# Channel norm once per token through memory, gates loaded a pair per slot, and residual tile loads on ScalarE's queue, in a hand-pipelined metaformer block

## What is computed

```python
def _ln_c(v, eps=1e-06):                 # over the 64 channels, per token
    m = jnp.mean(v, axis=1, keepdims=True)
    s = jnp.var(v, axis=1, keepdims=True)
    return (v - m) / jnp.sqrt(s + eps)

def _L0_conv_ref(x, ...):
    for s in (0, 2):
        xs = jnp.roll(x, (-s, -s), axis=(1, 2)) if s > 0 else x
        outs = [_window_attend(xh, ...) for xh in (xs[:, :32], xs[:, 32:])]
        if s > 0: outs = [jnp.roll(o, (s, s), axis=(1, 2)) for o in outs]
        results.append(jnp.concatenate(outs, axis=1))
    return results[0] + results[1]

# _window_attend: qkv = qkv_w @ xh; 4x4 windows, 8 heads of 4 channels;
#   softmax(q k^T * scale + bias) v + depthwise3x3(v)
x = x + _L0_conv_ref(_ln_c(x), qkv_w, lepe_w, bias_table)
t = tokens(x)
t = t + ffn(_ln_t(t))    # router softmax, top 2 of 8 experts, x @ expert_w + expert_b
```

## Time and profile before

| what | value |
|---|---|
| median of 3 runs | 3749.16 us (3746.48 to 3774.52) |
| the profiled execution | 3730.37 us |
| its span, first to last instruction | 3728.5 us |
| busy: TensorE, VectorE, GpSimd, ScalarE | 86%, 86%, 79%, 60% |
| mean granted TensorE clock | 0.923 of full speed |
| bytes moved by DMA | 432.05 MB, mean 116 GB/s |

### The profile page before, as it was taken

One profiled execution on the slowest core, in us unless ns is written; L12 is line 12 of the kernel. 1 busy time (PEld: TensorE's weight loads), 2 busy tenths in 40 slices (PEclk: granted clock), 3 DMA queues, 4 the chain that ended last, 5 costly groups with the idle time before them and its releaser, 6 DMA issues.

```text
span 3728.5 us, 203806 instructions
## 1 busy us (share of the span) xinstructions
PE 3199.5 (86%) x82757; PEld 1956.7 (52%) x82757; DVE 3190.4 (86%) x6174; ACT 2233.5 (60%) x4514; POOL 2942.7 (79%) x5385
## 2 busy tenths in 40 slices
PE   3889989988898888898889888888889888989884
PEld 1655555555555555555555555555555555555541
DVE  2789989998999989998889988888889988889983
ACT  2676666666666656665566656665556666666640
POOL 3988878888888878887788878877788878788860
PEclk8999999999999999999899999999899989999996
DMA  1245455555455545555545555545455545455545
GB/s 27 60 97 126 117 123 121 129 120 122 118 127 121 124 109 129 115 127 115 120 110 127 122 117 121 125 111 122 113 120 125 124 115 123 114 116 126 125 104 126
DMA packets 415302, 432.05 MB, mean 116 GB/s; under 512 B 129984, under 2 KB 395888, under 8 KB 414320
## 3 DMA queue, kind: packets, MB, share of 16 engines
q1 hardware_dynamic: 248432, 304.94, 36.0%
q0 software_dynamic: 165888, 113.57, 12.9%
HBM read 245.79 MB, written 58.98 MB: 82 GB/s over the span
## 4 chain that ended last, share of the span: by engine, by line
PE 36%; SPq 23%; issue 15%; DVE 14%; DMA 5%; ACT 3%; POOL 2%; DVEq 0%; ACTq 0%; POOLq 0%
SPq L397 13%; PE bank L628 8%; PE bank L564 7%; DVE lepe L899 4%; SPq L429 4%; PE bank L549 3%; PE bank L641 3%; PE bank L584 2%; SPq L455 2%; DVE gx L887 2%; PE bank L633 2%; DMA gate_rows<-gateT 2%; DVE row_max L907 2%; DMA z<-fin 2%; PE bank L653 2%
## 5 line engine op out<-in xcount | busy, mean ns | idle before, releaser
L504 POOL DMA_DIRECT2D vx<-vt x3072 | 1561.7, 517 | 414.1 <-PE bank L633 403.3
L628 PEld LDWEIGHTS bank<-probT,vx 128*32 128x32 f32 x36864 | 824.6, 189 | 464.5 <-issue 452.8
L628 PE MATMUL bank<-probT,vx 128*32 128x16 f32 x36864 | 886.3, 234 | 159.2 <-issue 144.0
L493 POOL DMA_DIRECT2D kx<-k_sb x1536 | 741.0, 489 | 229.5 <-issue 102.8
L564 PEld LDWEIGHTS bank<-kx,qx 32*32 32x32 f32 x36864 | 584.9, 110 | 443.6 <-issue 441.3
L564 PE MATMUL bank<-kx,qx 32*32 32x64 f32 x36864 | 689.3, 223 | 133.3 <-issue 111.1
L899 DVE SCALAR_TENSOR_TENSOR lepe<-vpad,lepe_sb,lepe 128x384 f32<-128x384 f32 x960 | 673.5, 702 | 0.8 <-issue 0.8
L718 ACT ACTIVATE prob<-prob 128x512 f32<-128x512 f32 x576 | 367.4, 638 | 288.1 <-DVE prob L912 285.0
L887 DVE TENSOR_TENSOR gx<-gate_wide,yn_pair 128x768 f32<-128x768 f32 x384 | 397.4, 1036 | 112.9 <-PE bank L549 62.1
L523 POOL TENSOR_TENSOR lepe_p<-lepe_p,tap_sb 128x384 f32<-128x384 f32 x384 | 434.9, 1133 | 32.7 <-issue 11.3
L912 DVE TENSOR_TENSOR prob<-bank,row_max 128x512 f32<-128x512 f32 x576 | 398.4, 692 | 16.7
(11 more groups left out here) (87 smaller groups left out, 4517.8 us busy)
## 6 DMA issues: line engine op xcount, KB each, us to landing
gate_wide<-gate_rows SPq DMA_DIRECT2D x384, 384.0 KB
vx<-vt POOLq DMA_DIRECT2D x3072, 12.0 KB
kx<-k_sb POOLq DMA_DIRECT2D x1536, 24.0 KB
yn_pair<-yn POOLq DMA_DIRECT2D x384, 96.0 KB
z<-fin SPq DMA_DIRECT2D x1344, 24.0 KB
xs<-in_x SPq DMA_DIRECT2D x96, 192.0 KB
xt<-in_x SPq DMA_DIRECT2D x192, 96.0 KB
z0t<-z SPq DMA_DIRECT2D x192, 96.0 KB
```

The lines of the kernel that those rows point to most:

```text
L493: pool.dma_start(kx[to + m:to + C:4, r % 2, m, :], k_sb[at + m:at + C:4, r % 2, :])\
L504: pool.dma_start(vx[to:to + TOK, r % 2, g * 8 + x:g * 8 + 8:2, odd, :], vt[at:at + TOK, r % 2, x::2, :, :].rearrange("p h n k -> p h (n k)"))\
L628: last = MM(bank_o[32 * c:32 * c + 32, at * TOK:(at + 1) * TOK], vx[:, kr % 2, :, at % 2, at // 2 * 4 + c], probT[:, kr % 2, at, c * TOK:( ...
```

## The change

Three things, and a new table of lags for them.

1. **Norm once per token.** `centre` and `variance` are stages of a tile now, on a tensor `xa` that holds each token once. The normalised tile goes to a memory tensor `xn` (`store_xn`, two DMAs), and `load_strips` reads both frames of xs from there (the same five DMAs as before, in another slot). That path takes nine slots, so every later stage's lag grows by nine or ten; `value` goes from 2 to 11, `tile_out` from 47 to 56.
2. **One pair's gates per slot.** `spread_gates` issues two DMAs of one expert pair in each of four slots (lag 49 to 52), the last of them in the slot before `products` (53); before, four DMAs in one slot three slots ahead. In SyncE's program it stands ahead of `store_z` now.
3. **Tile loads on ScalarE.** The block `load_tile` with its waits and seven DMAs moves from SyncE's program to ScalarE's, behind `tap_products` and ahead of `tile_variance`. Its lag is ten slots after `store_z` instead of nine: it comes one slot after the store that it waits for.

The core of the diff:

```diff
 LAG = dict(
-    centre=0, variance=1, value=2, query_key=3,
+    centre=0, variance=1, store_xn=2, load_strips=9, value=11, query_key=12,
...
-    store_z=15, load_tile=24, y_first=28, y_second=29, tile_sum=30, tile_variance=31, router=32, logits=33,
+    store_z=24, load_tile=34, y_first=37, y_second=38, tile_sum=39, tile_variance=40, router=41, logits=42,
...
+            def load_x(r, im):
+                for half in range(2):
+                    at = (r % IMT * (2 * SP) + half * SP) * W
+                    sp.dma_start(xa[half * C:(half + 1) * C, r % 2, :],
+                                 x_flat[bass.ds(im, 1)][:, :, at:at + SPX].rearrange("b c n -> c (b n)"))\
+                        .then_inc(x_loaded[r % 2], 16)
...
+                if ti := s.tile("store_xn"):
+                    k, r = ti
+                    wait_alone(sp, xn_made, k + 1)
+                    im = bass.ds(s.image(r, IMT), 1)
+                    for half in range(2):
+                        at = (r % IMT * (2 * SP) + half * SP) * W
+                        sp.dma_start(xn_flat[im][:, :, at:at + SPX].rearrange("b c n -> c (b n)"),
+                                     xa[half * C:(half + 1) * C, r % 2, :]).then_inc(xn_stored[r % 2], 16)
+                if ti := s.tile("load_strips"):
+
+                    k, r = ti
+                    if r % IMT == 0:
+                        wait_alone(sp, xn_stored[r % 2], (k // 2 + 1) * 32)
+                    if r % IMT < IMT - 1:
+                        wait_alone(sp, xn_stored[(r + 1) % 2], ((k + 1) // 2 + 1) * 32)
+                    if s.later(r, 2):
                         wait_alone(sp, k_made, (k - 1) * 2)
...
+                if (ti := s.in_tile("spread_gates")) and ti[2] < PAIRS:
+
+                    k, r, p = ti
+                    if p == 0:
+                        wait_alone(sp, gate_stored[r % 2], (k // 2 + 1) * 16)
+                    if s.later(r, 1):
+                        wait_alone(sp, gx_made, (k - 1) * PAIRS + p + 1)
+                    by_expert = gate_rows[r % 2].rearrange("(f p e) n -> e p f n", f=2, e=2)
+                    for odd in range(2):
+                        sp.dma_start(gate_wide[odd * C:(odd + 1) * C, p, :, :],
+                                     by_expert[odd, p].unsqueeze(0).broadcast_to([C, 2, SPX]))\
+                            .then_inc(gate_spread[r % 2], 16)
                 if st := s.strip("store_z"):
...
-                if ti := s.tile("spread_gates"):
-                    k, r = ti
-                    wait_alone(sp, gate_stored[r % 2], (k // 2 + 1) * 16)
-                    if s.later(r, 1):
-                        wait_alone(sp, gx_made, k * PAIRS)
...
@@ -755,6 +760,34 @@
                     S.activation(product.rearrange("p (r w) -> p r w", w=W), vrows(r, -1, j - 1), ACT.Copy,
                                  scale=lepe_sb[:, j:j + 1]).then_inc(tap_made, 1)
+                if ti := s.tile("load_tile"):
+                    k, r = ti
+
+                    if s.turn is None:
+                        last = min(2 * k + 4, N_STRIP)
+                        counts = [(last + 1) // 2, last // 2]
+                    else:
+                        counts = [k + 2, k + 2]
+                    for p in range(2):
+                        wait_alone(act, z_stored[p], counts[p] * (Z_DMAS * 16))
+                    if s.later(r, 2):
+
+                        wait_alone(act, y_made, k - 1)
...
+                    def put(dst, rows, at, src, row, n):
+                        act.dma_start(dst[rows, r % 2, at * W:(at + n) * W],
```

More of the change, by code:

```diff
@@ L213, in metaformer_block @@
         ebias_sb = sb("ebias_sb", [GE, 128])
+        xa = sb("xa", [128, 2, SPX])
         xs = sb("xs", [128, 4, SPX])
@@ L411, in slot @@
                                     put(1, 0, 0, half * HD, half * HD + 1, at + 22 + half * 8)
-                if ti := s.tile("load_tile"):
-                    k, r = ti
[L415 to L439, removed]
@@ L635, in slot @@
                     last.then_inc(pv_made, 1)
-                if st := s.strip("centre"):
-                    k, r = st
-                    pe.wait_ge(x_loaded[r // 2 % 2], (k // 4 + 1) * (X_DMAS * 16))
-                    if s.later(r, 1):
-                        pe.wait_ge(q_saved, k * 2)
-                    MM(bank_p[0][:, 0:SPX], const("centre"), xs[:, r % 4, :], start=True, stop=True).then_inc(xc_made, 1)
+                if ti := s.tile("centre"):
+                    k, r = ti
+                    pe.wait_ge(x_loaded[r % 2], (k // 2 + 1) * 32)
+                    if s.later(r, 2):
+                        pe.wait_ge(q_saved, (2 * k - 3) * 2)
+                    MM(bank_p[0][:, 0:SPX], const("centre"), xa[:, r % 2, :], start=True, stop=True).then_inc(xc_made, 1)
                 if ti := s.tile("tile_sum"):
@@ L698, in slot @@
                     S.activation(gateT[:, r % 2, :], bank_g[0:GE, 0:SPX], ACT.Copy).then_inc(gateT_saved, 1)
-                if st := s.strip("variance"):
-                    k, r = st
+                if ti := s.tile("variance"):
+                    k, r = ti
                     act.wait_ge(var_made, k + 1)
@@ L757, in slot @@
                                  scale=lepe_sb[:, j:j + 1]).then_inc(tap_made, 1)
+                if ti := s.tile("load_tile"):
+                    k, r = ti
+                    if s.turn is None:
[5 more added lines that the diff above has]
+                        wait_alone(act, z_stored[p], counts[p] * (Z_DMAS * 16))
+                    if s.later(r, 2):
+                        wait_alone(act, y_made, k - 1)
+                    t = (r + 1) % IMT
+                    im = bass.ds(s.image(r, IMT), 1)
+                    def put(dst, rows, at, src, row, n):
+                        act.dma_start(dst[rows, r % 2, at * W:(at + n) * W],
+                                     src[im][:, :, row * W:(row + n) * W]
+                                     .rearrange("b c n -> c (b n)")).then_inc(tile_loaded[r % 2], 16)
+                    for half in range(2):
+                        rows = slice(half * C, (half + 1) * C)
+                        put(xt, rows, 0, x_flat, t * (2 * SP) + half * SP, SP)
+                        put(z0t, rows, 0, z_flat[0], t * (2 * SP) + half * SP, SP)
+                    put(z2t, slice(0, C), 0, z_flat[1], (t * (2 * SP) + H - ROLL) % H, ROLL)
+                    put(z2t, slice(0, C), ROLL, z_flat[1], t * (2 * SP), SP - ROLL)
+                    put(z2t, slice(C, 2 * C), 0, z_flat[1], t * (2 * SP) + SP - ROLL, SP)
                 if ti := s.tile("tile_sum"):
```

97 lines of the change are left out of this document (45 added, 52 removed).

## The result

The changed kernel takes 4678.3 us (median of 4, 4674.49 to 4683.28), the one before 3747.82 us beside it: a ratio of 1.2467, with 95% interval 1.2405 to 1.2529. I had forecast 4420 us and slower; the direction and the mechanism hold, the size does not, and 4678 lies above my range.

A forecast was written before the change was run, and what follows sets the result against it. No engine was full; waits in a 37.5 us tile period bound the kernel. Loop +598, unrolled tiles +78, pipeline ends +10 and -5 on 3730.37 gave 4411, put at 4420 us; range 4120 to 4610 (66%), 4000 to 4610 with Rival 1 (80%).

The forecast's parts named there:

- Part (c): Tile loads and their wait for `z` on ScalarE ahead of `row_inv`: odd `fin` to `att` 18.1 us instead of 14.0.
- SyncE's chain: SyncE's queue from even `fin` to the odd `z` batch: `z` stores, x, xn, gates, output, strip loads; 21.3 us.
- VectorE's third leg: VectorE from even `fin` to the next odd `fin`, 17.2 us; as the tie it would give a 42.0 us period.
- The closed loop inside the Fori part: Even `fin` through SyncE, `z` landing, ScalarE and `att` back to itself: 45.8 us a tile against 37.5, over 72 tiles.
- second leg: VectorE from the start of `att` to the end of the even strip's `fin`: 6.7 us a tile.
- The unrolled parts: Tiles outside the Fori loop, `z` batches at 7.5 us: period 41.4 us instead of 37.5 for some 20 tiles, 78 us.
- the last gate piece: Spread issued behind the odd `z` batch: hidden in ScalarE's stall; without it, landed 12.6 us after `fin`, under 14.0.
- Part (a): Norm once per token: less TensorE, ScalarE and VectorE work in the first leg; alone worth 0.55 to 2.8 us a tile.
- Part (b): New SyncE queue, gate burst in four pieces: TensorE's issue idle falls, worth 0 to 2.7 us a tile; gate wait goes.
- Rival 1: DMA issues cheap on ScalarE, under 1 us for the seven tile loads: periods 41.9 and 37.5 us, 4050 us; 14%.
- Rival 2: TensorE's clock falls as well after each tile's stall, +3 us a tile: 4660 us; 12%.
- Rivals 3 and 4: ScalarE's `z` wait covered, relief wins: 3440 us, 4%; or a tie at 37.3 us a tile: 3750 us, 4%.

The follow-up runs named there:

- e1: The changed kernel with the tile loads and their waits back on SyncE, behind `store_z`; 4174.8 us (ratio 1.118).
- e3: The changed kernel with the tile loads one slot later on ScalarE (lag 35 instead of 34); 4186.7 us (ratio 1.122).
- e4: The changed kernel with ScalarE keeping its waits for `z` in slot 4 but SyncE issuing the tile loads; 4260.8 us (ratio 1.141).
- e2: The kernel before with only the tile loads moved to ScalarE, behind the tap product (lag 25 instead of 24); 4218.8 us (ratio 1.130).
- e6: e1 with the fourth gate piece issued together with the third, ahead of the odd `z` batch; 4102.8 us (ratio 1.093).
- e7: The kernel before with only the gate pieces: one pair in slots 40 and 41, two in 42, each ahead of `z`; 3792.1 us (ratio 1.012).
- e9: The kernel before with the tile loads on ScalarE at lag 26, in one lump at the end of the slot; 4214.1 us (ratio 1.125).
- e12: The kernel before with ScalarE tile loads split over four slots (lags 26 to 29) and stages from `y_first` one tile later; 3815.1 us (ratio 1.018).
- e11: The changed kernel with SyncE issuing the fourth gate piece only once the odd `z` batch has landed; 4673.7 us (ratio 1.247).

## Why the prediction was right or wrong

- **The mechanism, right.** Part (c) decides; the loop runs through SyncE's chain, the odd `z` batch, its landing, ScalarE's issues and `att`. e1 and e3 take it away, e4 splits it, e2 makes it from the kernel before. SyncE's chain and not VectorE's third leg sets when the odd batch starts: the odd batch starts 23.5 us after the even `fin`, VectorE's leg is 15.8.
- **The size, wrong.** "The closed loop inside the Fori part: ... = 45.8 us" failed. Over 66 tiles of the loop the terms are, in the order of the sum (forecast in brackets): chain 22.6 (21.3), `z` 9.1 (9.4), landing 3.3 (1.4), issues 4.4 (4.9), activations and start of `att` 2.15 (2.1), second leg 6.9 (6.7): 48.4 us. The largest error is the landing, +1.9 us. It was sized from one row, 1.4 us, where the mean over the loop before was already 1.8; why it is 1.5 us longer still in the changed kernel stays open. The chain is +1.3: xn stores and output are sometimes 2 to 2.8 us instead of 1.2 to 1.3 (1862.91 and 1866.86 above), and the landing of xn, which the sum had as covered, is waited for 0.5 us a tile (46.6 us in all).
- **The unrolled parts.** 41.4 us forecast; there the period is 43.5, and before it was 35.1 at the start and 37.0 at the end rather than 37.5. 72 x 10.9 = 785 and 20 x 7.4 = 148, with the +5 of the ends, make 3730 + 938 = 4668, and 4681 was measured.
- **The wait of `att`, 5 to 9 us a tile forecast, wrong by its own sum.** It measured 13.7. A period of 45.8 us less VectorE's 32.7 us of work leaves 13 us of waits, and the loop puts most of them ahead of `att`.
- **The range, wrong.** I worked out +980 us as an end and cut it to 4610 us "since then SyncE's chain gains slack". Nothing in the rows bears the cut; with a period of 45.8 plus the bounds of the landing (SyncE waited up to 4.2 us for z) the end is above 4650.
- **"if that goes, ... = 12.6 us from `fin` to its landing, under today's 14.0"**, the last gate piece: wrong. With the stall gone it is the next wait, 701 and 647 us in e1 and e3. The sum left out that the odd batch starts some 5 us late, and 14.0 was the first leg of one tile: over the loop before it is 12.4 us in the mean.
- **Part (a), 0.55 to 2.8 us a tile gained:** its saved work is real, but this estimate left out its own DMAs on SyncE, which stood only in the loop's chain; e6 against e7 puts them at 3.2 us a tile, which is argued and not isolated. **Part (b), 0 to 2.7:** the stops go, the time does not: 1.2% slower alone (e7).
- **Rival 1** (cheap issues) was wrong: 4.4 us for seven. The rule weighed with it, the Trainium skill's ("DMA: Bandwidth & Descriptors", Issuing engines are not separate DMA queues), says of the time to start a DMA that it "is usually small relative to the DMA itself". For each DMA alone the trace of the changed kernel agrees: about 0.5 us for the issue of a tile load in the median, 2.5 us until it has landed. My step from there to a price near nothing was wrong: seven starts in a row are 4.4 us of ScalarE's time, and in e9 they are the whole loss, 4.9 us a tile. **Rival 2** (clock): the level of 1.2 GHz was granted in the last 2 us of 63 of the 68 stalls looked at, but the second leg is 6.9 us in the mean against 7.1 over the loop before, so it cost nothing that shows. **Rivals 3 and 4** are out.

## What to carry to other kernels

An engine that is busy for only 60% of the time can have no room for a lump of DMA issues, if two other engines wait for it in turn: look not at its share but at the longest stretch between two things that others want from it; seven issues in a row cost their full length (4.3 us a tile in e4 against the changed kernel, 4.9 in e9), the same issues two at a time 0.7 us (e12). Before a wait is moved to another in-order engine, add up the loop that it closes, from the event back to itself, through the queue that has to release it. And where one queue issues for some 30 us of a 37.5 us period, what is saved elsewhere is paid back in its issues.

## What the runs showed of the hardware that I had not expected

- Seven DMA issues on ScalarE take 4.4 us in the mean (4.6 in the tile shown), on SyncE 4.9, and its activations wait for them.
- From the last issue of the same eleven stores to the load that waits for them it is 1.7 us in one kernel (e2) and 3.3 us in the changed one; 3.1 us with the next large transfer held back too (e11), while the DMA engines were 0.26 busy (2263.60 to 2266.40). The cause is open.
- TensorE's stops in mid stream ("issue") go with the DMA burst: 255 us with four gate transfers of 384 KB together, 90 us with the same bytes in pieces (e7).
